# A graph layer in two stages: message rows grouped by 512, and the first node groups prepared during the message stage

## What is computed

```python
h = relu(layernorm(x))                                   # (N, 128)
W_rel = einsum('rb,bdf->rdf', w_comp, weight)            # (32, 128, 128)
seg = etype * N + dst
agg = segment_sum(h[src] * norm, seg, 32 * N)            # (32, N, 128)
out = x + relu(einsum('rnd,rdf->nf', agg, W_rel) + h_bias + h @ loop_weight)
```

## Time and profile before

| | us |
|---|---|
| median of 3 runs | 1094.66 (1094.11 to 1096.1) |
| profiled execution | 1096.61 |
| its span | 1094.4 |

### The profile page before, as it was taken

One profiled execution on the slowest core, in us unless ns is written; L12 is line 12 of the kernel. 1 busy time (PEld: TensorE's weight loads), 2 busy tenths in 40 slices (PEclk: granted clock), 3 DMA queues, 4 the chain that ended last, 5 costly groups with the idle time before them and its releaser, 6 DMA issues. The chain is left out here.

```text
span 1094.4 us, 23539 instructions
## 1 busy us (share of the span) xinstructions
PE 1049.2 (96%) x4903; PEld 668.9 (61%) x4903; DVE 1027.7 (94%) x4358; ACT 933.7 (85%) x3253; POOL 808.6 (74%) x1381
## 2 busy tenths in 40 slices
PE   2999999999999999999999999998599999999997
PEld 1444444444444444444444444443599999999997
DVE  4999999999999999999999999998599999999995
ACT  5899999999999999999999999996488888888884
POOL 5788888888888888888888888883355555555553
PEclk9999999999999999999999999999699999999999
DMA  6122232232224222322232222221899999999993
GB/s 143 49 74 75 64 110 76 63 100 85 64 76 108 65 76 73 100 76 73 66 110 70 69 76 68 72 75 50 232 286 296 300 300 296 296 294 298 299 299 108
DMA packets 89570, 150.74 MB, mean 138 GB/s; under 512 B 18098, under 2 KB 57202, under 8 KB 89426
## 3 DMA queue, kind: packets, MB, share of 16 engines
q0 software_dynamic: 28224, 76.93, 24.4%
q1 hardware_dynamic: 59538, 71.49, 22.3%
q10 hardware_dynamic: 1664, 0.82, 0.4%
HBM read 97.68 MB, written 51.49 MB: 136 GB/s over the span
## 5 line engine op out<-in xcount | busy, mean ns | idle before, releaser
L612 PE MATMUL y_ps<-w_all,hT 128*128 128x512 f32 x1568 | 690.6, 593 | 0.6 <-DVE sum_a L762 0.6
L612 PEld LDWEIGHTS y_ps<-w_all,hT 128*128 128x128 f32 x1568 | 289.7, 190 | 331.1 <-issue 275.7
L397 POOL DMA_INDIRECT xg<-x,idx x392 | 394.9, 1007 | 77.1 <-issue 49.6
L486 ACT ACTIVATE z<-y_ps,mix 128x128 f32<-128x128 f32 x784 | 244.6, 363 | 62.6 <-PE y_ps L612 55.4
L762 DVE SCALAR_TENSOR_TENSOR sum_b<-y_ps,mix,sum_b 128x128 f32<-128x128 f32 x784 | 266.4, 340 | 0.0
L371 POOL TENSOR_TENSOR u<-z 128x128 f32<-128x128 f32 x392 | 181.8, 464 | 42.0 <-ACT z L486 37.8
L435 POOL DMA_DIRECT2D out<-res x98 | 75.6, 771 | 135.0 <-DVE res L971 135.0
L577 ACT ACTIVATE hw<-xw,shift,nrstd 128x128 f32<-128x128 f32 x392 | 161.5, 482 | 2.1 <-DVE shift L962 0.4
L661 PE MATMUL y_ps<-w_loop,hwT 128*128 128x128 f32 x782 | 152.6, 277 | 0.0
L662 PE MATMUL y_ps<-seg,pick 96*128 96x128 f32 x782 | 152.6, 276 | 0.0
L664 PE MATMUL y_ps<-seg,pick 97*128 97x128 f32 x782 | 152.5, 276 | 0.0
(11 more groups left out here) (92 smaller groups left out, 1205.4 us busy)
## 6 DMA issues: line engine op xcount, KB each, us to landing
seg<-msgs SPq DMA_DIRECT2D x391, 96.8 KB, 3.9
msgs<-msg SPq DMA_DIRECT2D x98, 258.0 KB
xw<-x POOLq DMA_DIRECT2D x97, 256.0 KB, 5.6
out<-res POOLq DMA_DIRECT2D x97, 256.0 KB, 4.7
type_bc<-type_rows SPq DMA_DIRECT2D x28, 224.0 KB, 5.5
xg<-x,idx POOLq DMA_INDIRECT x392, 2.6
w_all<-weight ACTq DMA_DIRECT2D x1, 512.0 KB
dst_i<-dst ACTq DMA_DIRECT2D x1, 196.0 KB, 3.0
```

Of the source, the lines that this page charges most:

```text
L397: nc.gpsimd.indirect_dma_start(xg[:, q, j, :], None, x, bass.IndirectOffsetOnAxis(ap=idx[:, q, j:j + 1], axis=0)).then_inc(s_gather[q * G ...
L486: ins = nc.scalar.activation(z[:, r, b, :], y_ps[r][:, b, :], ACT.Copy, scale=mix[:, q, j, b:b + 1])
L612: nc.tensor.matmul(y_ps[r][:, b0:b0 + B // 2, :], hT[:, q, j, :], w_all[:, b0:b0 + B // 2, :], start=True, stop=True).then_inc(done, 1)
```

## The change

Messages: group g now holds the edges 512 g to 512 g + 511, partition p has the edges 512 g + 4 p to 512 g + 4 p + 3, and a store writes 512 rows that follow one another. `src`, `norm`, the types and a new input of destinations (`dst_cols`, loaded into `dst_c`, integers) are laid out so. The old `dst` stays for counting. The destination column is copied from `dst_c` in place of `dst_f`. A small table `early_tab` is added in `first_rows`.

Node groups 0 to 7: their segments are loaded by SP after the stores of message groups 70 to 77, four loads each, after a wait for the first four stores of each of the three slots. x of groups 0 and 1 is loaded by POOL in its steps 66 and 68, x of groups 2 to 4 between its last two steps and of 5 to 7 after them. For groups 0 and 1 (EARLY), single steps of statistics, means, root, reciprocal, shift, relu, `rel` and `pick` (in halves) are appended to the steps of the message stage. The last groups of TensorE and ScalarE are interleaved with the transposes and copies of groups 0 and 1. The slices `win_ps` are taken from the two `y_ps` tiles that are free first. The flag is stored after message group 2 and read before the last step. The diff, cut to its core:

```diff
+EARLY = 2
+PREP = 28
+MODE_STORE = 2
-        win_ps = [y_ps[0][:, 0:G, :], y_ps[1][:, 0:G, :], y_ps[2][:, 0:G, :], y_ps[0][:, G:2 * G, :]]
+        free_first, free_next = (NT - 3) % RING, (NT - 2) % RING
+        win_ps = [y_ps[free_first][:, 0:G, :], y_ps[free_first][:, G:2 * G, :],
+                  y_ps[free_next][:, 0:G, :], y_ps[free_next][:, G:2 * G, :]]
@@ SP
+            sp.dma_start(dst_c[:, :], dst_cols).then_inc(s_dst_c, 16)
-                sp.dma_start(msg_rows[:, bass.ds(g * (G * C), G * C)],
+                sp.dma_start(msgs[g * G * P:(g + 1) * G * P, :].rearrange("(p t) c -> p (t c)", t=G),
+            for g in range(NG):
                 store_messages(g, g // RING, g % RING)
+                if g == MODE_STORE:
+                    sp.wait_ge(s_start, 1)
+                    sp.dma_start(mode, mode_i[:, :]).then_inc(s_table, 16)
+                if g == NG - PREP:
+                    for q in range(RING):
+                        sp.wait_ge(s_stored[q], 16 * 4)
+                if 0 <= g - (NG - PREP) < LRING:
+                    early = g - (NG - PREP)
+                    load_windows(early, early, early_tab, n_seg[early])
@@ POOL
-                nc.gpsimd.tensor_copy(msg[:, q, :, F:C], dst_f[:, bass.ds(g * G, G)].unsqueeze(2)).then_inc(s_dst_col, 1)
+                nc.gpsimd.tensor_copy(msg[:, q, :, F:C], dst_c[:, bass.ds(g * G, G)].unsqueeze(2)).then_inc(s_dst_col, 1)
+            def early_windows(s):
+                if s in (0, 2):
+                    ask_x(s // 2)
+                if s in (PREP - 6, PREP - 4):
+                    g = (s - (PREP - 6)) // 2
+                    pool.wait_ge(n_seg[g], 16 * G)
+                    relative(g, 0, g, n_rel)
+                early_windows(g - (NG - PREP - 4))
             gathers(NG, NG // RING, NG % RING)
+            for g in range(EARLY, LRING // 2 + 1):
+                ask_x(g)
             gathers(NG + 1, (NG + 1) // RING, (NG + 1) % RING)
+            for g in range(LRING // 2 + 1, LRING):
+                ask_x(g)
+            pool.wait_ge(s_table, 16)
+            compact = pool.value_load(mode, min_val=0, max_val=1)
             for t in range((NG - 1) * G, NT):
                 add_pair(t, t % RING)
@@ ScalarE
+            def early_windows(s):
+                if s in (11, 12):
+                    window_std(s - 11, s - 11)
+                if 18 <= s < 18 + EARLY * G:
+                    g, j = (s - 18) // G, (s - 18) % G
+                    if j == 0:
+                        act.wait_ge(n_shift, g + 1)
+                    ins = window_relu(g, j)
+                    if j == G - 1:
+                        ins.then_inc(n_h, 1)
+                early_windows(g - (NG - PREP))
-            for j in range(G):
-                scale_bases(NG - 1, (NG - 1) % RING, j)
+            scale_bases(NG - 1, (NG - 1) % RING, 0)
+            window_hT(0, 0)
+            scale_bases(NG - 1, (NG - 1) % RING, 1)
+            scale_bases(NG - 1, (NG - 1) % RING, 2)
+            window_hT(1, 1)
+            scale_bases(NG - 1, (NG - 1) % RING, 3)
@@ TensorE
+            pe.wait_ge(s_table, 16)
+            compact = pe.value_load(mode, min_val=0, max_val=1)
             pe.wait_ge(s_hT_sb, NG)
-            for j in range(G):
-                products(NG - 1, (NG - 1) % RING, j)
-            pe.wait_ge(s_table, 16)
+            window_transposes(0, 0)
+            products(NG - 1, (NG - 1) % RING, 0)
+            products(NG - 1, (NG - 1) % RING, 1)
+            pe.wait_ge(s_mix, NG)
+            window_transposes(1, 1)
+            products(NG - 1, (NG - 1) % RING, 2)
+            products(NG - 1, (NG - 1) % RING, 3)
@@ window_sums
+                else:
+                    pe.wait_ge(s_a, 2 * (NT - 2 + g // 2))
@@ VectorE
+                nc.vector.tensor_scalar(early_tab[:, :], start[:, 0:LRING * G], float(EARLY_ROWS - SEG), None, ALU.min)
+            def early_windows(s):
+                if 0 <= s < EARLY * G:
+                    window_stats(s // G, 0, s // G, range(s % G, s % G + 1))
+                elif s in (8, 9):
+                    window_means(s - 8, s - 8)
+                elif s in (13, 15):
+                    window_rstd((s - 13) // 2, (s - 13) // 2)
+                elif s in (14, 16):
+                    window_shift((s - 14) // 2, (s - 14) // 2)
+                elif s == PREP - 4:
+                    window_rows(0, 0, 0, G // 2)
+                elif s == PREP - 3:
+                    window_rows(0, 0, G // 2, G).then_inc(n_pick, 1)
+                elif s == PREP - 1:
+                    window_rows(1, 1, 0, G // 2)
+                elif s == PREP:
+                    window_rows(1, 1, G // 2, G).then_inc(n_pick, 1)
+                early_windows(g - (NG - PREP))
             step(NG - 1, (NG - 1) // RING, (NG - 1) % RING)
+            dve.wait_ge(s_table, 16)
+            compact = dve.value_load(mode, min_val=0, max_val=1)
             step(NG, NG // RING, NG % RING)
-            for g in range(2):
-                window_stats(g, 0, g, range(G))
-                window_means(g, g)
-                window_rstd(g, g)
-                window_shift(g, g)
-            for g in range(2):
-                window_rows(g, g)
             sweep(dve, NGW - 2, node_step, LRING, LRING, 1)
@@ host
+    def group_cols(name, pad):
+        return edge_row(name, pad).reshape(tiles // G, P, G).transpose(1, 0, 2).reshape(P, tiles)
```

More of the change, by code:

```diff
@@ L318, in store_messages, with load_windows @@
                 sp.wait_ge(s_dst_col, g + 1)
-                sp.dma_start(msg_rows[:, bass.ds(g * (G * C), G * C)],
+                sp.dma_start(msgs[g * G * P:(g + 1) * G * P, :].rearrange("(p t) c -> p (t c)", t=G),
                              msg[:, q, :, :].rearrange("p t c -> p (t c)")).then_inc(s_stored[q], 16)
[L322 to L326, removed]
-                store_messages(g, g // RING, g % RING)
+            def load_windows(g, q, table, done, full=G, last=0):
+                windows = full + (last > 0)
+                _, rows = nc.values_load_multi_w_load_instructions(
+                    table[0:1, bass.ds(g * G, windows)], (mybir.EngineType.SP,), min_val=0, max_val=ROWS - SEG,
+                    skip_runtime_bounds_check_because="first_row is clamped to EP - SEG or counts compacted rows")
+                for j, row in enumerate(rows):
+                    sp.dma_start(seg[0:SEG_P, q, j, :, :].rearrange("p c f -> p (c f)"),
+                                 msgs[bass.ds(row, SEG), :].rearrange("(p c) f -> p (c f)", c=CHUNKS)
+                                 ).then_inc(done, 16)
+            for g in range(NG):
+                store_messages(g, g // RING, g % RING)
+                if g == MODE_STORE:
[7 more added lines that the diff above has]
+                    load_windows(early, early, early_tab, n_seg[early])
+            sp.wait_ge(s_table, 16)
+            compact = sp.value_load(mode, min_val=0, max_val=1)
             for q in range(RING):
                 sp.wait_ge(s_stored[q], 16 * len(range(q, NG, RING)))
-            sp.wait_ge(s_table, 16)
-            with sp.If(sp.value_load(mode, min_val=0, max_val=1) > 0):
+            with sp.If(compact > 0):
                 with sp.Fori(0, NW + 2) as w:
@@ L341, in _, with reload_windows @@
                     hold(sp, passed["sp"])
[L344 to L357, removed]
+                sp.wait_ge(n_rel, EARLY)
+                for q in range(LRING):
+                    sp.wait_ge(n_seg[q], 16 * G)
+                    load_windows(q, q, row_tab, c_reload)
+            def reload_windows(g, n, q, full=G, last=0):
+                sp.wait_ge(n_res, g - (LRING - 1))
+                load_windows(g, q, row_tab, n_seg[q], full, last)
+            sweep(sp, NGW - 1, reload_windows, LRING, LRING, LRING)
             g = NGW - 1
-            load_windows(g, g // LRING, g % LRING, LAST_FULL, LAST)
+            reload_windows(g, g // LRING, g % LRING, LAST_FULL, LAST)
         @block.gpsimd
@@ L428, in _ @@
                     pool.wait_ge(c_st, t * 16 + 16)
+                pool.wait_ge(c_reload, LRING * G * 16)
+                pool.wait_ge(n_pick, EARLY)
+                for g in range(EARLY):
+                    relative(g, 0, g, c_rel)
+                pool.wait_ge(c_pick, EARLY)
             def store_results(g, q, full=G, last=0):
@@ new lines, in window_stats, with window_rows @@
+            def window_stats(g, n, q, tiles, x_loads=1):
+                r = q % NRING
+                if 0 in tiles:
+                    dve.wait_ge(n_x[q], n * 16 + 16 * x_loads)
+                for j in tiles:
+                    nc.vector.bn_stats(nstats[:, r, j, :], xw[:, q, j, :]).then_inc(n_bn, 1)
+            def window_rows(g, q, first=0, windows=G):
+                r = q % NRING
+                if not is_before(g, NRING):
+                    dve.wait_ge(n_y, g - (NRING - 1))
+                dve.wait_ge(n_rel, g + 1)
+                return picks(r, first, windows)
```

(15 more changed lines are left out.)

156 lines of the change are left out of this document (76 added, 80 removed).

## The result

| | before | changed |
|---|---|---|
| median, us | 1095.38 (4 runs) | 1082.12 (1082.03 to 1083.85, 4 runs) |
| profiled execution, us | 1096.61 | 1083.85 |
| its span, us | 1094.4 | 1082.1 |

The ratio is 0.9885, 95% interval 0.9873 to 0.9897. The changed kernel is 13.3 us faster by the medians (11.3 to 13.9 by the interval) and 12.3 by the two spans. The forecast was 11.7. Of the 1.0 between these two gains, 0.4 lies outside the span: all four runs of the changed kernel are 1.75 to 1.83 us longer than their spans, those of before 2.1 to 2.3. No run shows why. The profiled execution of the changed kernel is also the longest of its four, that of before is 1.2 above its median, so the spans are good for where the time went, the medians for how much.

What follows compares the result with a forecast made beforehand. TensorE paces both stages and time is lost in the seam between them; 12.2 us gained there less 0.5 at the start is 11.7, from the median 1094.66 to 1083.0 us, range 1079 to 1087.5 (8 in 10).

Steps and rivals of the forecast that it cites:

- T3: Start of TensorE's transposes of node group 3, where steady pace begins; forecast to move from 790.02 to 777.8 us.
- steps 1, 5: VectorE's last message ended at 763.35 us before; group 2 takes 5.2 to 5.3 behind its new end, transposes at 772.4.
- the start: Kernel start: the added 0.2 MB load costs 0.4 us, the small table of early rows on VectorE 0.1.
- S: Delay gathered in the message stage by the added work: 2.3 us, with ends at 0 and 9.8.
- Steps 2 and 3: Delays to VectorE's end: two times four transposes between the last products, +0.94 us; half pick of group 1, +0.6.
- step 6: TensorE idles 5.4 us after the sums of group 0; at half clock the next work takes 5.43 in place of 3.12.
- Two-input rule: Picks beside POOL's adds: VectorE and GpSimd exclude each other; each of four could cost 0.46 us more, 1.8 in all.
- The layout: Stores of 512 consecutive rows in place of 128 strips: no time, bound 0 both ways.
- A: Message-stage additions hide almost wholly, or the half clock is shorter: 1081.0, or 1079.8 with half the clock's loss saved; chance 0.17.
- B: Message stage pays fully, POOL and VectorE holding each other up, above all at the last tiles: 1086.7 to 1087.7; chance 0.16.
- C: POOL's destination copy from integers slows every group, deciding from +0.12 us a group; 1107.5 at 7.73 a group; chance 0.03.
- D: Early segments arrive late because SP's loads stand behind stores, so the change of stages gains nothing: about 1097; chance 0.02.

Runs made afterwards that it cites:

- experiment 4: The changed kernel with the early segment loads of groups 2 to 7 left to after the last store: 1088.70 us.
- experiment 5: The changed kernel with the x requests of groups 2 to 7 moved behind POOL's last pair: 1084.51 us.
- experiment 6: The changed kernel with the eight early relus moved from the end of ScalarE's step into its wait in the scaling of the fourth tile: 1081.83 us.
- experiment 7: The changed kernel with the picks of groups 0 and 1 made whole, in one step each, in place of two halves: 1083.85 us.
- experiment 9: The changed kernel with the 0.2 MB load of integer destinations issued only after the first gathers have landed: 1082.57 us.
- experiment 2: The changed kernel with 42 identity transposes on TensorE between the sums of group 0 and the transposes of group 2: 1080.37 us.
- experiment 11: The kernel before, unchanged, profiled a second time: transposes of group 3 start 36.20 us behind the last message group's mix matmul (38.41 in the first profile).
- experiment 12: The kernel before with only the new row layout, profiled again: transposes of group 3 start 34.61 us behind the last message group's mix matmul (36.00 first).
- experiment 1: The kernel before with only the new row layout, integer destination column and its load: 1093.77 us against 1095.77, ratio 0.9977.
- experiment 8: The changed kernel with group 2 also normalised in the message stage, relus in ScalarE's gap, VectorE's work reordered and 16 identity transposes: 1078.16 us.
- experiment 3: The changed kernel with TensorE's sums of group 1 taken before the transposes of group 2: 1082.66 us.

## Why the prediction was right, step by step

- *What bounds it and that T3 follows VectorE's end* (steps 1, 5): right. Experiments 4 and 5 show that with segments or x late, it is these that it waits for. VectorE ended at 767.01 and group 2 began at 771.85. The forecasts, 767.2 and 772.4, leave out the start, which had a term of its own; with the start's 0.5 they are 767.7 and 772.9. So VectorE's end was 0.7 early, since S was smaller, and group 2 came 4.84 behind it in place of 5.2. Steps 2 and 3: each four transposes moved the products on by 0.44, and the half pick is 0.68 long.
- *Half clock* (step 6): idle 5.15 (5.4). The next group took 5.83 in place of 5.43, which takes back 0.4 of what was early. This part is luck: over six profiles, the changed kernel and experiments 4, 5, 6, 7 and 9, that group took 4.69 to 5.98. Experiment 2 shows the price.
- *S*: 2.3 forecast, 1.66 found, made up otherwise. The half picks of steps 24 and 25 cost 0.5, the third nothing (1.0 for the three). Statistics and means cost nothing (0.3). x requests cost 0.14 and 0.20 (0.5 with the offsets). The last tiles cost nothing (0.5), and TensorE's register load neither: products end by their pace at 756.10, the transposes begin at 756.11. That agrees with the Trainium skill (Advanced Engine Details and Errata, Engine Queue Depths), by which TensorE has a queue of 64 instructions; no run shows apart that the queue is what hid the load. ScalarE's eight relus, which I had put at 0 (0.8 at most) because it is idle 8% of the time, cost 0.8. This is the term that was wrong in kind: a share of idle time says nothing of what is queued behind. ScalarE's gap lies inside the scaling of the third and fourth tile, and the relu was put ahead of the scaling of the first, for which VectorE waits (experiment 6).
- *Two-input rule* (the Trainium skill, SBUF — State Buffer, Who interferes with whom): the 1.8 us that I worked out from it did not come, since the four half picks took 0.67 to 0.68, and 0.66 was the estimate without POOL. The rule itself is not contradicted. Two of the four had next to nothing of POOL's beside them that reads SBUF: one nothing, one the last 0.1 us of a cast. Beside the other two it was POOL's instruction that grew: an index copy took 0.85 us (0.25 in the middle of the stage), and the longest of three offsets 0.65 (the shortest 0.20). VectorE and POOL at the first of the four, in the changed kernel:

```profile
734.58 0.85 POOL L436 COPY idx<-src_all 128x4 int32<-128x4 int32 x1
...
734.70 0.68 DVE L932 TENSOR_TENSOR pick<-iota_n,rel 96x512 f32<-96x512 f32 x1
```

- *The start*: 0.5 forecast and 0.51 in the two profiles. But experiment 9 shows that this is within what M2 varies by. The load was not shown to cost anything, so that the number fits is luck.
- *The layout*: "no time" is not borne out; by the timed runs the kernel before gains 2 us (experiments 11 and 12).
- *Rivals*: A was nearest in size, B fell by experiment 5, C by experiment 1, D by the trace.

The seam gained 14.5 us; less the start's 0.5 and the stage's 1.66 that is the 12.3 between the spans. A seam of before can be 2.2 shorter (experiment 11) and one of the changed kernel 1.1 shorter (experiment 9), so the size of 14.5 holds to about 2 us. No run takes away the early normalisation of groups 0 and 1, the transposes between the last products or the early flag by itself; that these carry what experiment 4 leaves is argued from the order of the chain.

## What to carry to other kernels

Find the one start after which everything is a fixed pace, and follow what the in-order engines have queued ahead of it; the gain within the span is the shift of that start and nothing else. Small steps slipped into a stage paced by another engine are free up to the lag that it is seen to bear, here 0.3 us a group on VectorE, but where in the step they stand matters more than how idle the engine is on average. A head start for the engine that paces is in part lost again (1.7 of 6.2 us in experiment 8) unless the next slowest has its work moved too.

## What the hardware showed that I had not expected

- An idle stretch of 2.48 us was enough for TensorE's half clock (1.2 GHz), as one of 5.15 us was: the granted clock was 1.00 in 770 to 771, 0.61 in the next us, and 0.50 behind it (experiment 3). Work without use in the idle stretch kept it at 2.4 GHz (granted clock 1.00) and won 2.7 us of trace, 1.75 by the medians (experiment 2).
- Eight single statistics of 0.28 us in eight groups that VectorE fills to 98% (195.78 of 200 us) made no group longer than 7.48 us.
- The start of a kernel varies by 1.5 us with the same instructions (M2 40.16 to 41.71; 39.84 and 41.29 in two profiles of one kernel). Why is not shown. Differences below that are to be read between landmarks of one trace, not from the times.
